# A vision tower in one launch: the patch stage re-ordered and its first norm folded into the embedding weights

## What is computed

```python
patches = x.reshape(B, C, h, P, w, P).transpose(0, 2, 4, 3, 5, 1)
patches = patches.reshape(B, h * w, P * P * C)           # 36 x 768
y = _layernorm(patches, ln1_w, ln1_b)
y = jnp.einsum('bnp,pd->bnd', y, lin_w) + lin_b
y = _layernorm(y, ln2_w, ln2_b)
y = jnp.concatenate([cls, y], axis=1) + pos_embedding[:, :n + 1]
```

## Time and profile before

| | |
|---|---|
| time, three runs | 307.93 (307.88 to 312.0) us, median first |
| the profiled execution | 312.02 us, span 310.3 us |
| PE, PEld busy | 256.7 us (83%), 209.4 us (67%) |
| DVE, ACT, POOL busy | 207.4 us (67%), 95.2 us (31%), 43.4 us (14%) |
| mean granted TensorE clock | 0.922 |
| chain that ended last | PE 63%, DVE 18%, SP's queue 7%, ACT 6% |
| loads | 12.08 MB in 16147 packets, mean 39 GB/s |

### The profile page before, as it was taken

One profiled execution on the slowest core, in us unless ns is written; L12 is line 12 of the kernel. 1 busy time (PEld: TensorE's weight loads), 2 busy tenths in 40 slices (PEclk: granted clock), 3 DMA queues, 4 the chain that ended last, 5 costly groups with the idle time before them and its releaser, 6 DMA issues.

```text
span 310.3 us, 5533 instructions
## 1 busy us (share of the span) xinstructions
PE 256.7 (83%) x2188; PEld 209.4 (67%) x2188; DVE 207.4 (67%) x495; ACT 95.2 (31%) x226; POOL 43.4 (14%) x76
## 2 busy tenths in 40 slices
PE   1058899978879899999999989998769799927596
PEld 1037786777868657777776988786548576707484
DVE  0679187715845549788888935777587747996931
ACT  0045003422243561111112226467312334826000
POOL 6023001000540100000000004499000000000000
PEclk9999797997558999999999969999999999977699
DMA  7943002940000170000000000000000000000001
GB/s 174 305 76 70 2 0 67 309 137 2 2 2 2 46 262 0 2 0 0 0 2 1 0 0 2 3 3 2 0 3 0 2 0 0 0 2 1 0 34 44
DMA packets 16147, 12.08 MB, mean 39 GB/s; under 512 B 4603, under 2 KB 15578, under 8 KB 16122
## 3 DMA queue, kind: packets, MB, share of 16 engines
q1 hardware_dynamic: 13864, 10.01, 11.8%
q10 hardware_dynamic: 2258, 1.73, 1.9%
HBM read 11.13 MB, written 0.61 MB: 38 GB/s over the span
## 4 chain that ended last, share of the span: by engine, by line
PE 63%; DVE 18%; SPq 7%; ACT 6%; issue 4%; DMA 1%; ACTq 0%; DVEq 0%
PE bank L1623 46%; PE bank L2091 5%; SPq L466 3%; PE bank L1752 3%; DVE part L1467 2%; PE bank L1785 2%; PE bank L1816 2%; DVE big L1531 1%; DMA cols<-in_L_attn_factor 1%; PE bank L1727 1%; DVE keys_n L1512 1%; DVE big L1049 1%; PE bank L1860 1%; ACT xT L703 1%; DVE big L1565 1%
## 5 line engine op out<-in xcount | busy, mean ns | idle before, releaser
L1623 PE MATMUL bank<-xT,big 128*128 128x296 f32 (+1 forms) x192 | 45.7, 391 | 0.0
L1623 PEld LDWEIGHTS bank<-xT,big 128*128 128x128 f32 x192 | 34.4, 190 | 9.4 <-issue 0.2
L1618 PE MATMUL bank<-ident,ones 128*128 128x128 f32 x108 | 18.4, 339 | 8.1 <-POOL queries_n L543 6.4
L1623 PE MATMUL bank<-xT,fT 128*128 128x296 f32 (+12 forms) x96 | 24.6, 416 | 0.6 <-DVE xT L1488 0.6
L1623 PE MATMUL bank<-big,cur 128*128 128x256 f32 (+1 forms) x100 | 23.3, 382 | 0.7 <-DVE cur L1242 0.7
L1618 PEld LDWEIGHTS bank<-ident,ones 128*128 128x128 f32 x108 | 17.4, 250 | 9.3 <-POOL queries_n L543 6.4
L785 ACT ACTIVATE cen<-bank 128x296 f32<-128x296 f32 x20 | 8.3, 418 | 46.4 <-PE bank L1623 40.7
L1623 PEld LDWEIGHTS bank<-xT,fT 128*128 128x128 f32 x96 | 17.2, 191 | 7.0 <-issue 2.1
L1623 PEld LDWEIGHTS bank<-big,cur 128*128 128x128 f32 (+1 forms) x100 | 18.1, 182 | 4.9 <-DVE cur L1242 1.5
L1255 DVE SCALAR_TENSOR_TENSOR h<-bank,route,h 128x256 f32<-128x256 f32 (+1 forms) x40 | 16.9, 478 | 3.2 <-PE bank L1623 3.2
L1623 PE MATMUL bank<-big 128*128 128x256 f32 (+1 forms) x60 | 16.8, 449 | 1.9 <-DVE big L1049 1.9
(11 more groups left out here) (293 smaller groups left out, 495.7 us busy)
## 6 DMA issues: line engine op xcount, KB each, us to landing
big<-in_x SPq DMA_DIRECT2D x3, 576.0 KB, 11.1
big<-in_L_ffn_w_gate SPq DMA_DIRECT2D x2, 512.0 KB, 5.7
big<-in_L_ffn_w_up SPq DMA_DIRECT2D x2, 512.0 KB, 6.5
big<-in_L_ffn_w_down SPq DMA_DIRECT2D x1, 1024.0 KB, 8.4
big<-in_L_tok_lin_w SPq DMA_DIRECT2D x3, 256.0 KB, 9.9
small<-in_L_ffn_w_gate SPq DMA_DIRECT2D x1, 768.0 KB, 5.2
small<-in_L_ffn_w_up SPq DMA_DIRECT2D x1, 768.0 KB, 6.8
small<-in_L_ffn_w_down SPq DMA_DIRECT2D x1, 768.0 KB, 8.0
```

The lines of the kernel that those rows point to most:

```text
L1618: pe.matmul(b[:, 0:P], ones[:, :], ident[:, :], start=True, stop=True)
L1623: ins = pe.matmul(out_, a_, b_, start=(n == 0), stop=(n == len(pairs) - 1))
```

## The change

The images are turned as they land, without having been normalised. ACT and POOL copy the six windows of a channel out of `img` into `patches[c]`, in the order that the transposes want (ACT two, POOL four); PE turns one channel after another; ACT alone empties these banks, by plain copies.

The first norm is folded. With rate r and mean m of a token, (x - m) r w W + b W is r (x W') + c, where W' is w W less its column mean (written `lin_w * ln1_w - mean_row`) and c is b W plus the bias. So PE makes column sums (`("cs",)`), spreads them to all partitions (`("mr",)`, `("cr",)`), DVE centres the six pieces of `lin_w`, and the rate of each token comes from `rstd` by one more small product (`("rt",)`) and a reduction on DVE. The rate and c are applied in one DVE operation for each tile out of PSUM; the second norm's four operations become two for each tile.

The order also changes. The expert weights have a place of their own in memory and are issued behind the other loads, not behind the embedding, except the two down matrices. All attention weights are issued by SP. Two large clearings of POOL move behind the windows. The small matrices move behind the last embedding tile on PE and into the layer norm on DVE. Composed weights move behind the first attention, v1 and o1 behind the experts.

The diff, cut to its core (`...` marks what is left out):

```diff
@@ memory @@
-        patches = cut(big, XI)
-        lin_w = cut(big, 6 * D).rearrange("p (k n) -> p k n", k=6)
-        at[0] = 2 * QK
         w_eg = cut(big, KD * NE * EI).rearrange("p (k e i) -> p k e i", k=KD, e=NE)
+        patches = [v[0:96, :, :].rearrange("p a b -> p (a b)").rearrange("p (n e) -> p n e", n=NG) for v in fT]
...
@@ SP @@
             for c in range(NC):
                 sp.dma_start(imv[0:96, c, :], im[c]).then_inc(images_in[c], 16)
+                if c == 0:
+                    for n in range(NC):
+                        sp.dma_start(lin_w[:, 2 * n:2 * n + 2, :], lw[n]).then_inc(patch_w_in, 16)
...
-            filled(sp, ("y", 2))
             for k in range(KD):
                 rows = slice(k * P, (k + 1) * P)
                 sp.dma_start(w_eg[:, k, :, :], ...).then_inc(moe_in, 16)
...
+            filled(sp, ("y", 4))
             sp.dma_start(w_ed, i["L0_ffn_w_down"].rearrange("e p n -> p e n")).then_inc(moe_in, 16)
@@ POOL @@
+            pool.tensor_copy(token_of, ident[0:T, 0:T]...).then_inc(consts_ready, 1)
...
+            for c in range(NC):
+                pool.wait_ge(images_in[c], 16)
+                for w in range(POOL_WINDOWS):
+                    pool.tensor_copy(patches[c][:, w, :]..., pv[:, c, :, w, :]).then_inc(windows_pool, 1)
             pool.memset(fprobsT[:, :, :], 0.0)
@@ ACT @@
+            b = take(act, ("ln",))
+            empty(act.copy(ln_cols..., b[:, 0:4 * NC]))
+            for t in range(TT):
+                b = take(act, ("ad", t))
+                empty(act.copy(addend[:, t, :], b[:, 0:DA]))
+            windows(0)
+            channel(0)
+            b = take(act, ("cs",))
+            empty(act.copy(col_sums, b[:, 0:4]))
+            b = take(act, ("mr",))
+            empty(act.mul(mean_row, b[:, 0:D], 1.0 / PV))
+            for c in (1, 2):
+                windows(c)
+                channel(c)
             act.wait_ge(consts_ready, N_CONSTS)
             inverse_root(96, slice(0, NG))
@@ DVE @@
+            def centred_weights(k):
+                dve.scalar_tensor_tensor(out=lin_w[:, k, :], in0=lin_w[:, k, :], scalar=ln_cols[...],
+                                         in1=mean_row, op0=ALU.mult, op1=ALU.subtract).then_inc(weights_centred, 1)
+            channel_statistics(0)
+            channel_statistics(1)
+            emptied(dve, ("mr",))
+            emptied(dve, ("ln",))
+            for k in range(4):
+                centred_weights(k)
+            link(channel_statistics(2))
...
+            variance_given(embedded(0), spread_small_weights)
+            placed(0)
+            embedded(1).then_inc(var_ready, 1)
+            embedded(2).then_inc(var_ready, 1)
+            dve.wait_ge(rstd_ready, 3)
+            placed(1)
+            dve.wait_ge(rstd_ready, 4)
+            stats = placed(2)
+            roots[0] = 4
+            layer_norm(2, stats, small_matrices)
@@ PE @@
+            bs_ = [fill(("y", t)) for t in range(2)]
+            for k in range(PK):
+                pe.wait_ge(weights_centred, k + 1)
+                for g in range(2):
+                    emptied(pe, ("xp", k, g))
+                for t in range(2):
+                    ins = pe.matmul(bs_[t][:, 0:D], patT[:, k, t * P:(t + 1) * P], lin_w[:, k, :], ...)
...
+            embedding((2, 3))
+            embedding((4,))
+            small_matrices()
+            pe.wait_ge(attn_w_in, 16 * N_ATTN_W)
```

## The result

The changed kernel takes **322.63 us** (median of four runs, 321.8 to 323.25); the kernel before took 308.96 (307.88 to 312.0). The ratio is 1.042, 95% interval 1.034 to 1.051: the change makes the kernel slower. The prediction said 300.4, and its range ended at 306.0.

What follows compares the result with a forecast made beforehand. It took serial loading (column loads first), statistics, normalising and turning ahead of the embedding as the bound, with ACT setting the new stage. Terms -7.7 + 0.9 + 0.3 - 1.0 = -7.5 took 307.93 to 300.4 us; range 295.2 to 306.

Steps and rivals of the forecast that it cites:

- from constants to the table: Start of the patch stage: PE does fillers 3.0, tiny turns 0.3 and table products 4.65 us from 4.3, through at 12.2.
- Channels landing at 12.5 to 13: Image loads: 2.56 MB at 256 GB/s takes 10 us from about 2.5, so the last channel lands at 12.5 to 13.
- Column sums 3.0: PE ahead of the mean row: 12 products of two columns, priced from a one-column row, take 3.0 us, to 16.7.
- Rival 2: Patch stage: the PE, ACT, DVE loop for the mean row is the new bound, giving 306.5 us; chance 0.12.
- ACT sets the stage: Patch stage: ACT's window copies and bank emptying run to 24.4, so the embedding starts at 23.0 against 31.97.
- First pair 7.1: Start of the embedding: 12 products for the first two token tiles take 7.1 us, ready at 30.1; bounds 28.1 and 33.2.
- Pair to turning 18.9: From first tile pair to turning for the first attention: 18.9 us, turning at 49.0; before it was 17.6.
- Behind the turning, +0.2: After turning starts: 0.9 lost to moved v1 and o1 turns, 0.3 lost behind the attention, 1.0 won on experts' loads.
- The stall of 1.9: PE's 1.94 us "issue" wait at the query products: moving experts' loads wins 0 to 1.94, taken as 1.0 us.
- Attention weights late: Behind the embedding: all attention weights share SP's queue and come too late, turning at 54.3, 305.7 us; chance 0.07.
- Low clock into the attention: From column sums into the first attention: PE stays at low clock, turning at 65.6, 326 us; chance 0.07.
- The median: Whole kernel: the 7.5 us won, from a profiled execution of 312.0, is taken off the median 307.93, giving 300.4.

Runs made afterwards that it cites:

- spread run: Changed kernel with position rows loaded as 32 and 5 rows and the two broadcast rows sent to 48 partitions, not 37: median 312.07 us.
- last kernel: Changed kernel with table loads split 32/5 and broadcast to 48, the patch stage reordered, and both powers moved behind the attention scores: median 300.04 us.
- reordered kernel: Changed kernel with table loads split 32/5 and broadcast to 48, plus early ACT windows, statistics first and table products later: median 306.86 us.
- 47 rows: Changed kernel with position rows loaded as 32 and 5 rows, but the two broadcast rows sent to 47 partitions: median 322.25 us.
- experts late: Changed kernel with the expert loads issued in their old place, behind the last embedding fill: median 322.07 us.
- powers late: Changed kernel, loads and order otherwise untouched, with the two powers moved behind the attention scores: median 317.22 us.

## Why the prediction was wrong, by its steps

**The step that failed** is the one from constants to the table: "PE from 4.3: six filler products ... three tiny turns 0.3, then the five table products ... PE is through at 12.2". It prices the products and never asks when the table is there. The three loads on ACT's queue were taken as landed because they are small, while the images got a sum in bytes over GB/s. In the kernel before, `make_table` stood behind the last statistics, so nothing in its trace showed these loads late; moving the first reader ahead of a load's landing makes the landing a term of the sum. Measured: products done at 26.00, not 12.2. Of the 18.25 us by which the turning (67.25) missed the forecast (49.0), 13.8 are here. The spread run shows 10.6 of time hanging on it.

**Channels landing at 12.5 to 13**: channel 1 was there at 15.12 and channel 2 at 16.66, while fifteen of their sixteen parts had landed by 11.21 and 13.22. The rate of 256 GB/s was a mean over sixteen engines, and an image is there when its last part is. POOL's twelve copies then took 0.36 each, the short price (4.4 us in all), in the spread kernel also beside DVE's statistics.

**Column sums 3.0**: 5.17, at 0.215 an instruction. Rival 2 took 0.26, nearer than the forecast's 0.125, which came from products of one column at a recorded clock of 1.00. These sums ran ahead of the first record of the clock, at PE's early pace (last section); where part of them had full clock, in the last kernel, they took 3.78. With the rest of the way to the mean row (34.55 against 17.8) this adds 2.9 to the 13.8.

**ACT sets the stage**: not quite. Its copies were cheaper than I took them (0.56, not 0.67), and PE's last three transposes stood 1.75 for the constant row's bank, eight fills behind in the ring, which DVE emptied behind the third statistics. I counted copies and not the ring. Mean row to embedding took 5.8, forecast 5.2. The sum so far, 13.8 + 2.9 + 0.6 = 17.3, is the delay of the embedding, 40.37 - 23.0.

**First pair 7.1**: 7.06, and the clock over it 0.76, the same as before the change. Right.

```profile
40.40:47.40 7.00, 7.00 (x28) 5.87 (x27) 0.00 (x0) 0.96 (x3) 0.00 (x0) 0.76 0.01 2
```

**Pair to turning 18.9**: 19.8. The mechanism is right, the small matrices and powers in a row; the powers took 1.65 each and not 0.73. That they cost the gain of the folded norm was in the sum; that they need not stand there was not seen, and was worth 5.4 by itself.

**Behind the turning, +0.2**: measured -0.4 (253.2 against 253.6). The eight turns of v1 and o1 took 0.87 more on the chain, as forecast 0.9:

```profile
183.70 2.78 PE L1973 MATMUL bank<-ident,small 128*128 128x128 f32 x24
186.32 1.04 PE L1803 MATMUL bank<-ident,small 128*128 128x128 f32 x8
```

The stall of 1.9 went whole, where I took half. The reason I gave was PE's instruction fetch behind the experts' loads; the time of the packet speaks for the fetch, and no run decides on the loads.

**The rivals.** Attention weights late: no; the stage never waited for them. Low clock into the attention: the clock was 0.66 over 60 to 70. There the powers took 1.65 each and not the 0.94 of the kernel before, which is more than the 0.9 above; the query products behind them had 1.00 (70.3 to 78.7) and took 8.36 us for 256 instructions. The time behind the turning is unchanged, so it is not the cause, though the result ended on that rival's side. Mean-row loop: real, but the smaller part. With the table out of the way the embedding still came at 30.8 and not at 23, and the reordering that takes the loop out from behind the table brought 5.2 us of median.

**The median.** I subtracted a term measured in one profiled execution (312.02) from a median 4.1 lower. The differences of spans (+10.2) and of medians (+13.7) show that a difference of two profiled executions doesn't carry over to medians by itself: the changed kernel's profiled execution was as its timed ones, that of the kernel before was not.

## What to carry to other kernels

Before moving a reader of small loads to the front of an engine's order, find when they land and by how many engines they come: a row count of 37 or 47 instead of 48 and 32 cost 10 us here. Then move it only so far that nothing else queues behind it; moving the reader of the late loads back brought 7.4 of these 10 us with the loads untouched. Work whose result is needed late belongs in a later idle stretch, and not ahead of the hand-over that everybody waits for.

## What was not expected of the hardware

Slow loads seem to hurt others: 111 rows of 1 KB took 17 us to land, and beside them one part in sixteen of two images of 576 KB came 3.9 and 3.4 us behind the rest. Channel 1, the median of the three, took 11.8 us to land instead of 8.3.

A clock of 1.00 in a view can mean that the trace has no record. In the changed kernel the first record of the clock lies at 37.06 us, and ahead of it the view counts full speed. (In the kernel before it lies at 26.55, so that the 1.00 of 6.4 to 19 in the earlier trace rows is no reading either.) Over 20 to 24 the view reads 1.00 while an instruction of the table products takes 0.475 us (4.75 for 10); in the last kernel, at a recorded 1.00 behind the first pair, it takes 0.265 (1.59 for 6). The column sums of the reordered kernel read 1.00 at 5.17 us, with the first record at 27.53; those of the last kernel read 0.70 at 3.78 us, with the first record at 7.29.

The first pair tells which of the two levels (1.2 and 2.4 GHz) PE had until then. Its 24 instructions at 0.2125 us each (5.1 us for 24 at 1.00) behind the first record and at twice that ahead of it give, as an estimate, the middle row below.

| us | spread | 47 rows | experts late | powers late | reordered |
|---|---|---|---|---|---|
| first record of the clock | 33.39 | 42.29 | 44.70 | 45.76 | 27.53 |
| first pair, estimate | 6.4 | 6.4 | 7.6 | 7.6 | 7.8 |
| first pair, measured | 6.64 | 6.64 | 7.83 | 7.88 | 8.13 |

So PE ran at the lower level until the first record. Why that lies at 7.29 in one execution and at 27.53 in another, of programs that are the same up to there, is open. A duration from another place in the trace is a price at that place's clock, and the clock is known only from its first record on.

The stall of 1.9 us called "issue" amid the query products is in every kernel with the old patch stage and in none with the new one. A late packet of instructions goes with it each time; what makes the packet late is open.
